# Where VectorE's small work stands: block table one unit tile later, first batch's routing and halving behind a product

## The chip, the cores and the metric

The kernel runs on one core of one Trainium2 chip. The metric is the device time of one execution in microseconds; the median of several runs counts. Matrix products run on TensorE, elementwise work and reductions on VectorE, activations and many casts on ScalarE, some elementwise work and the indirect transfers on GpSimd, and most transfers are issued by SyncE (SP).

## The reference, cut to what matters

The input x has 4 batches of 512 rows of 512 numbers; a context has 4 batches of 512 rows of 256. Cross attention is added to x, and then a mixture-of-experts layer, both behind a layer norm:

```
x = x + xattn(layernorm(x), ctx)     # softmax((ctx Wq+bq)(ctx Wk+bk)^T), times the normed rows
x = x + ffn(layernorm(x))
# ffn(h): logits = h gate_w^T; top 2 of 8 experts by softmax, weights renormalized
#   routed : sum over the 2 experts of  w * (silu(h Wg) * (h Wu)) Wd      (inner width 352)
#   shared : sigmoid(h sgw) * (silu(h Sg) * (h Su)) Sd                    (inner width 1408)
```

## The kernel before, in words

Numbers are split into a high and a low half of 16 bits, and each product takes three matmuls per chunk (high-high, high-low, low-high), so a product of 128 x 512 over a depth of 512 is 12 matmuls.

Up to about 48 us the attention of batches 0 and 1 is computed. Then `ffn_block(t)` runs the shared expert for t = 0 to 3, one batch each, in 11 unit tiles j of 128 columns. For each tile TensorE does the gate product (gate(j)), the up product (up(j)) and, for the tile two before, the down product (down(j-2)). ScalarE applies the SiLU to the gate; VectorE multiplies it with the up product (`product(j)`, L1313); ScalarE casts the high half (L869) and VectorE subtracts for the low half (`low_part`, L1318). TensorE's up(j+1) waits for product(j), since both use one bank. Behind the four blocks come 39 blocks of 128 routed rows each (`expert_product`, `expert_down`), whose rows come back from DRAM sorted by expert; GpSimd adds each block's result to the output by an indirect transfer (L657).

Each engine walks through its own program in order. Everything that isn't the shared expert is hung on points of this walk: the tables `AT_POINT_FIRST` (t = 0), `AT_POINT` (t = 1 and 2) and `AT_POINT_LAST` (t = 3) map (j, "gate" | "up" | "down") to stages, and the same tables are read by every engine, which does its part of the stage there and leaves out stages in which it has no part. On VectorE the order within tile j is: stages of "gate", product(j), stages of "up", low_part(j), stages of "down".

The stages that matter here:

- `logits_before` in block 0: TensorE's 32 small matmuls for the router of batch 0, VectorE's `read_logits` (L1026), ScalarE's exponential, VectorE's `route` (L1036, some twenty small instructions that choose the top two experts and write the weights beside the rows).
- `x_low` in block 0: VectorE scales the last rows of batch 1's attention (L982) and makes four low halves `x_low(1, c)` (L961) from banks of PSUM. TensorE's `turn_attn(1, c)` (L1433, 16 transposes behind up(1)) writes the same banks, each group of four behind its x_low, and VectorE's `attn_low` (L987) reads them.
- `halves_before`: ScalarE's `halve_high(0)` (L752) and VectorE's `halve_low(0)` (L1015) make the two halves of batch 0's normed rows, which GpSimd's `send_rows(0)` scatters to DRAM.
- `assign`: TensorE's small sums of the routing mask and VectorE's row numbers.
- `tables` in block 3: VectorE's three parts (L1120 to L1173) of the table that tells which rows and which expert each of the 39 blocks has. Part 2 releases `table_ready` and `pads_ready`; GpSimd then sends eight pads (L627), and SP loads the first blocks behind those.
- pieces: the routed experts' weights are loaded in 24 pieces through three places of SBUF (a piece's load waits until the piece before in its place has been taken over), cast by ScalarE (`piece_hi`, L845) and subtracted by VectorE (`piece_low`, L1287). `PIECES_AT` sets them beside the tiles, in block 3 two per tile from 4 at (0, "gate") to 15 at (5, "down"), then one per tile. Pieces of one point come behind the stages of that point.

Of the kernel before, what the change touches and what calls it, by code (L numbers as in the profile page):

```python
# [48 lines left out]

AT_POINT_FIRST = {  # L50
    (0, "gate"): [("logits_before", 0)],
    (0, "up"): [("x_low", 0)],
    (0, "down"): [("halves_before", 0)],
    (1, "gate"): [("attn_lows", 0)],
    (1, "up"): [("attn", 0), ("attn", 1), ("attn", 2), ("attn", 3)],
    (1, "down"): [("assign", 0)],
    (2, "gate"): [("mix", 0), ("mix", 1), ("mix", 2), ("mix", 3)],
    (2, "up"): [("stats2", 0)],
    (3, "gate"): [("norm2", 0)],
    (3, "up"): [("halves", 0)],  # L60
    (8, "up"): [("logits", 0)],
# [3 lines left out]

AT_POINT_LAST = {
    (0, "up"): [("assign", 0)],
    (1, "gate"): [("tables", 0)],
    (1, "down"): [("tables", 1)],
    (2, "gate"): [("tables", 2)],  # L70
}


# [22 lines left out]
def at_point(t):  # L96
    return (AT_POINT_FIRST, AT_POINT, AT_POINT, AT_POINT_LAST)[t]
# [6 lines left out]
def build_xattn_moe(nc, x, ctx_in, w_q, b_q, w_k, b_k, gate_w, w_gate, w_up, w_down,  # L104
# [66 lines left out]
    with ExitStack() as stack:  # L171
# [15 lines left out]
        def att_bank(b, stage, i):  # L187

            if stage == "h":
                return bank[(2, 0, 1, 3)[i]]  # L190
            if four_banks(b, stage):
                return bank[b * 4 + (2 if stage == "qk" else 0) + i]
            return bank[1] if stage == "assign" else bank[i % 2]
# [735 lines left out]
        def _(dve):  # L929
            def statistics(which, b):  # L930

                if which == 1:
                    dve.wait_ge(added, RT * b + RT)
                    nc.vector.memset(carrier[:, 1:2], 0.0)
                for i in range(RT):
                    op = nc.vector.bn_stats(stats[:, which, i, :], row_tile(b, i))  # L936
                op.then_inc(stats_done[which], 1)
                variance(which, b)
# [25 lines left out]
            def row_max(b, n):  # L964
                dve.wait_ge(energy_done, RT * b + n + 1)
                nc.vector.tensor_reduce(neg_max[:, n:n + 1], att_bank(b, "energy", n)[:, :], AX.X, ALU.max,
                                        negate=True).then_inc(max_ready, 1)
# [50 lines left out]
            def step(op, b, k):  # L1018

                op.then_inc(r_step, 1)  # L1020
                dve.wait_ge(r_step, ROUTE_STEPS * b + k)

            def over_tile(a):
                return a[:, :].unsqueeze(2).broadcast_to([P, RT, E])

            def read_logits(b):  # L1026
                dve.wait_ge(logits_done, b + 1)
                parts = att_bank(b, "logits", 0)[:, 0:RT * 3 * NL].rearrange("p (t a e) -> p t e a", t=RT, a=3)
                nc.vector.tensor_reduce(logits[:, :, :], parts, AX.X, ALU.add).then_inc(logits_read, 1)
                dve.wait_ge(logits_read, b + 1)  # L1030
                step(nc.vector.tensor_reduce(top[:, :], logits[:, :, 0:E], AX.X, ALU.max), b, 1)
                nc.vector.tensor_scalar(exp_in[:, :, E], logits[:, :, E], -1.0, None, ALU.mult)
                nc.vector.tensor_tensor(exp_in[:, :, 0:E], logits[:, :, 0:E], over_tile(top),
                                        ALU.subtract).then_inc(exp_in_ready, 1)

            def route(b):  # L1036

                dve.wait_ge(r_exp, b + 1)
                nc.vector.tensor_scalar(gate_den[:, :], exp_out[:, :, E], 1.0, None, ALU.add)
                step(nc.vector.tensor_reduce(soft_sum[:, :], exp_out[:, :, 0:E], AX.X, ALU.add), b, 2)  # L1040
                nc.vector.reciprocal(gate_val[:, b, :], gate_den[:, :])
                step(nc.vector.reciprocal(soft_inv[:, :], soft_sum[:, :]), b, 3)
                step(nc.vector.tensor_tensor(probs[:, :, :], exp_out[:, :, 0:E], over_tile(soft_inv), ALU.mult), b, 4)

                p_other = probs[:, :, :].unsqueeze(2).broadcast_to([P, RT, E, E])
                p_own = probs[:, :, :].unsqueeze(3).broadcast_to([P, RT, E, E])
                nc.vector.tensor_tensor(greater, p_other, p_own, ALU.is_gt)
                step(nc.vector.tensor_tensor(equal, p_other, p_own, ALU.is_equal), b, 5)
                step(nc.vector.tensor_tensor(equal.rearrange("p t e j -> p t (e j)"),
                                             equal.rearrange("p t e j -> p t (e j)"),  # L1050
                                             before[:, :, :].rearrange("p e j -> p (e j)").unsqueeze(1)
                                             .broadcast_to([P, RT, E * E]), ALU.mult), b, 6)
                step(nc.vector.tensor_tensor(greater.rearrange("p t e j -> p (t e j)"),
                                             greater.rearrange("p t e j -> p (t e j)"),
                                             equal.rearrange("p t e j -> p (t e j)"), ALU.add), b, 7)
                step(nc.vector.tensor_reduce(rank[:, :, :], greater, AX.X, ALU.add), b, 8)
                nc.vector.tensor_scalar(mask[:, :, :], rank[:, :, :], TOP_K - 0.5, None,
                                        ALU.is_lt).then_inc(mask_ready, 1)
                step(nc.vector.scalar_tensor_tensor(out=chosen[:, :, :], in0=rank[:, :, :], scalar=TOP_K - 0.5,
                                                    in1=probs[:, :, :], op0=ALU.is_lt, op1=ALU.mult), b, 9)  # L1060
                step(nc.vector.tensor_reduce(top_sum[:, :], chosen[:, :, :], AX.X, ALU.add), b, 10)
                step(nc.vector.reciprocal(top_inv[:, :], top_sum[:, :]), b, 11)
                if b == 0:
                    dve.wait_ge(const_ready, 1)
                nc.vector.tensor_copy(hx[b % 2][:, :, TOKEN:XW],
                                      const_f[:, TOKENS][:, b * RT:(b + 1) * RT].unsqueeze(2)
                                      .broadcast_to([P, RT, XW - TOKEN]))
                step(nc.vector.tensor_tensor(hx[b % 2][:, :, META:META + E], chosen[:, :, :], over_tile(top_inv),
                                             ALU.mult), b, 12)
# [167 lines left out]
            def attention(t, j, point):  # L1237

                b = t + 1
                for stage, i in at_point(t).get((j, point), ()):  # L1240
                    if stage == "stats1":
                        statistics(0, b)
                    elif stage == "norm1":
                        normalize(0, b)
                    elif stage == "energy":
                        row_max(b, i)
                    elif stage == "x_halves":
                        x_row_halve(b)
                    elif stage == "inverse":
                        for n in range(RT):  # L1250
                            inverse_sum(b, n)
                    elif stage == "attn_low":
                        attn_row_low(b, i)
                    elif stage == "attn_lows":
                        for c in range(KC):
                            attn_low(b, c)
                    elif stage == "mix":
                        add_mix(b, i)
                    elif stage == "stats2":
                        statistics(1, b)  # L1260
                    elif stage == "norm2":
                        normalize(1, b)
                    elif stage == "logits":
                        read_logits(b)
                    elif stage == "x_low":
                        scale_attn(b, RT - 1)
                        for c in range(KC):
                            x_low(b, c)
                    elif stage == "logits_before":
                        read_logits(b - 1)  # L1270
                        route(b - 1)
                    elif stage == "halves":
                        halve_low(b)
                    elif stage == "halves_before":
                        halve_low(b - 1)
                    elif stage == "assign":
                        assign(b - 1)
                    elif stage == "tables":
                        tables(i)
                    elif stage == "route":  # L1280
                        route(b)
# [453 lines left out]
```

## Time and profile before

| | |
|---|---|
| time before, median of 3 runs | 689.49 us (689.24 to 690.12) |
| the profiled execution | 687.42 us |
| its span, first to last instruction | 685.7 us |
| mean granted TensorE clock | 0.987 of 2.4 GHz |
| VectorE busy | 300.5 us (44%) |
| ScalarE busy | 228.6 us (33%) |
| GpSimd busy | 161.0 us (23%) |

Times of rows are microseconds from the first instruction. TensorE's own rows are of two kinds, PE (matmuls) and PEld (weight loads). A row of a timeline merges like instructions that follow one another: start, length, engine, line, operation, output and inputs, count, and in brackets the idle time before it and what ended it.

### The profile page before, as it was taken

The numbers are of one execution on the slowest core, as the hardware profiler recorded it, in microseconds if no ns is written. First come the engines' busy times: TensorE is split into PE (matmuls) and PEld (weight loads), VectorE is DVE, ScalarE is ACT, GpSimd is POOL, SyncE is SP. The second block draws the span as 40 slices with busy tenths as digits, with TensorE's granted clock in tenths as the row PEclk, the third lists the DMA queues.
The fourth block names the chain that finished last, engine by engine and source line by source line (L and its number), as shares of the span: only waits on it lengthen the run. The fifth ranks groups of instructions, "written<-read, shape, count | busy, mean of one in ns | idle before, by whom it ended". The sixth has DMA issues, their size and how long they took to land.

```text
span 685.7 us, 10319 instructions
## 1 busy us (share of the span) xinstructions
PE 652.5 (95%) x3426; PEld 332.2 (48%) x3426; DVE 300.5 (44%) x703; ACT 228.6 (33%) x341; POOL 161.0 (23%) x134
## 2 busy tenths in 40 slices
PE   8889999999999999999999799999999999999990
PEld 5544444444444444444444344455555555555550
DVE  3899554525524445523559763452222222222220
ACT  3445053313710223620345353332223222223220
POOL 2560280005000004000435700013222222222221
PEclk9999999999999999999999999999999999999995
DMA  9531097222420314430367987348888888888852
GB/s 279 182 92 47 12 307 224 85 93 110 101 39 0 63 32 156 96 60 0 61 210 264 282 276 169 105 117 128 131 128 132 134 129 135 135 126 139 122 72 31
DMA packets 146899, 85.77 MB, mean 125 GB/s; under 512 B 109721, under 2 KB 131481, under 8 KB 146850
## 3 DMA queue, kind: packets, MB, share of 16 engines
q1 hardware_dynamic: 134722, 56.25, 36.0%
q0 software_dynamic: 10544, 27.30, 17.9%
q10 hardware_dynamic: 1584, 1.57, 0.7%
q8 instruction: 31, 0.51, 0.3%
q14 instruction: 18, 0.15, 0.1%
HBM read 32.76 MB, written 27.29 MB: 88 GB/s over the span
## 4 chain that ended last, share of the span: by engine, by line
PE 70%; issue 10%; DMA 7%; DVE 7%; SPq 1%; POOLq 1%; ACT 1%; POOL 1%; ACTq 0%
PE bank L1593 30%; PE bank L1608 16%; PE bank L1641 9%; PE bank L1668 6%; PE bank L1450 5%; DMA out<-staging,token_blk 4%; DMA hidden<-hT 2%; PE bank L1407 2%; DMA arena<-x 1%; PE bank L1416 1%; POOLq L652 1%; DVE arena L955 1%; DVE stats L936 1%; DVE arena L1287 1%; POOL out L657 1%
## 5 line engine op out<-in xcount | busy, mean ns | idle before, releaser
L1593 PE MATMUL bank<-hT,arena 128*128 128x512 f16 x1056 | 238.0, 379 | 5.7 <-DVE prod L1313 4.8
L1593 PEld LDWEIGHTS bank<-hT,arena 128*128 128x128 bf16 x1056 | 102.5, 98 | 132.0 <-DVE prod L1313 6.2
L1641 PE MATMUL bank<-arena,hx_odd 128*128 x936 | 146.0, 313 | 0.0
L1608 PE MATMUL bank<-arena,hidden 128*128 128x512 bf16 x528 | 120.3, 379 | 0.0
L1641 PEld LDWEIGHTS bank<-arena,hx_odd 128*128 128x128 f16 x936 | 91.1, 98 | 53.8 <-issue 0.9
L657 POOL DMA_INDIRECT out<-staging,token_blk x39 | 60.8, 1558 | 165.1 <-ACT staging L913 139.0
L1350 DVE TENSOR_TENSOR prod<-silu_sb,bank 128x352 f32<-128x352 f32 x39 | 20.3, 521 | 150.7 <-PE bank L1641 150.7
L1668 PE MATMUL bank<-arena,hidden 128*128 (+1 forms) x351 | 82.3, 379 | 4.1 <-DMA hidden<-hT 2.5
L1608 PEld LDWEIGHTS bank<-arena,hidden 128*128 128x128 bf16 x528 | 51.3, 98 | 63.0 <-issue 2.3
L875 ACT ACTIVATE silu_sb<-bank 128x512 f32<-128x512 f32 x44 | 26.2, 596 | 112.1 <-PE bank L1593 112.0
L1313 DVE TENSOR_TENSOR prod<-silu_sb,bank 128x512 f32<-128x512 f32 x44 | 30.1, 684 | 75.4 <-PE bank L1593 71.3
L869 ACT CAST hidden<-prod 128x512 bf16<-128x512 f32 x44 | 27.0, 618 | 88.9 <-DVE prod L1313 88.9
L1668 PEld LDWEIGHTS bank<-arena,hidden 128*128 128x128 bf16 (+1 forms) x351 | 34.2, 98 | 41.8 <-issue 7.2
L913 ACT ACTIVATE staging<-bank,w_blk 128x512 f32<-128x512 f32 x39 | 26.8, 687 | 64.6 <-PE bank L1668 64.6
L1318 DVE TENSOR_TENSOR hidden<-prod,hidden 128x512 bf16<-128x512 f32 x44 | 35.0, 799 | 28.7 <-ACT hidden L869 28.5
L609 POOL TENSOR_TENSOR rstd<-var_eps,minus_half 128x4 f32<-128x4 f32 x8 | 9.7, 1207 | 155.7 <-DVE var_eps L949 155.5
L1450 PE MATMUL bank<-arena 128*128 128x512 f16 x192 | 43.1, 379 | 0.0
L901 ACT CAST hT<-prod 128x352 bf16<-128x352 f32 x38 | 18.4, 484 | 63.5 <-DVE prod L1350 63.5
L1287 DVE TENSOR_TENSOR arena<-staging,arena 128x1408 bf16<-128x1408 f32 (+1 forms) x14 | 23.5, 1680 | 15.5 <-ACT arena L845 15.3
L1450 PEld LDWEIGHTS bank<-arena 128*128 128x128 f16 x192 | 18.8, 98 | 23.0 <-issue 0.6
L845 ACT CAST arena<-staging 128x1408 bf16<-128x1408 f32 (+1 forms) x18 | 25.0, 1396 | 9.8 <-DMA staging<-L_ffn_w_gate 7.1
L892 ACT ACTIVATE silu_sb<-bank 128x352 f32<-128x352 f32 x39 | 18.1, 463 | 28.9 <-PE bank L1641 28.9
(190 smaller groups left out, 506.3 us busy)
## 6 DMA issues: line engine op xcount, KB each, us to landing
staging<-L_ffn_w_gate SPq DMA_DIRECT2D x6, 704.0 KB, 4.9
staging<-L_ffn_w_up SPq DMA_DIRECT2D x6, 704.0 KB, 5.9
arena<-x SPq DMA_DIRECT2D x3, 1024.0 KB, 7.4
out<-arena POOLq DMA_DIRECT2D x3, 1024.0 KB, 4.8
staging<-L_ffn_w_down SPq DMA_DIRECT2D x6, 512.0 KB, 3.8
staging<-L_ffn_sw_gate SPq DMA_DIRECT2D x11, 256.0 KB, 3.3
staging<-L_ffn_sw_up SPq DMA_DIRECT2D x11, 256.0 KB, 3.9
staging<-L_ffn_sw_down SPq DMA_DIRECT2D x11, 256.0 KB, 4.5
```

The costliest lines, as they stand in the source:

```text
L657: nc.gpsimd.indirect_dma_start(out=out[:, :], out_offset=bass.IndirectOffsetOnAxis(ap=token_blk[:, k:k + 1], axis=0), in_=yblk[:, k % 2, : ...
L869: nc.scalar.copy(hidden[:, j % 3, HI, :], prod[:, j % 2, :]).then_inc(hid_hi, 1)
L875: nc.scalar.activation(silu_sb[:, :], gate_ps[:, :], ACT.Silu).then_inc(silu_ready, 1)
L913: nc.scalar.activation(yblk[:, k % 2, :], bank[4 + k % 2][:, :], ACT.Copy, scale=w_blk[:, k:k + 1]).then_inc(y_ready, 1)
L1287: nc.vector.tensor_tensor(arena[:, at + gap:at + gap + n], piece_space[piece_slot(q)][:, 0:n], arena[:, at:at + n], ALU.subtract).then_inc ...
L1313: nc.vector.tensor_tensor(prod[:, j % 2, :], silu_sb[:, :], up_ps[:, :], ALU.mult).then_inc(prod_ready, 1)
L1318: nc.vector.tensor_tensor(hidden[:, j % 3, LO, :], prod[:, j % 2, :], hidden[:, j % 3, HI, :], ALU.subtract).then_inc(hid_lo, 1)
L1450: op = nc.tensor.matmul(att_bank(b, "mix", i)[:, :], place(b).xnT[:, xp, c, i * P:(i + 1) * P], place(b).attnT[:, ap, c, :], start=(c == 0 ...
L1593: op = nc.tensor.matmul(ps[:, :], weights[:, j, wp, kind, c * P:(c + 1) * P], hT[:, t % 2, hp, c, :], start=(c == 0 and s == 0), stop=(c = ...
L1608: op = nc.tensor.matmul(out_ps[i][:, :], hidden[:, j % 3, hp, i * P:(i + 1) * P], weights[:, j, wp, DOWN, :], start=(j == 0 and s == 0), s ...
L1641: op = nc.tensor.matmul(ps[:, 0:I], xT[:, k % X_SLOTS, xp * KC + c, :], arena[:, bass.ds(at + (part_at(0, part) + wp * low_gap(part) + c * ...
L1668: op = nc.tensor.matmul(ps[:, :], hidT[0:n, k % 3, hp, c * P:(c + 1) * P], arena[0:n, bass.ds(at + (DOWN_AT + wp * DN + c * H), H)], start ...
```

## The change

The first batch's `route` becomes a stage of its own, `route_before`, and moves from in front of product(0) to behind it, ahead of `x_low`. The halving of batch 0's rows moves from the end of tile 0 to the end of tile 2, for ScalarE and VectorE both. In the last block the three parts of the table move: part 0 from (1, "gate") to (1, "down"), part 1 from (1, "down") to (2, "down"), part 2 from (2, "gate") to (3, "down"). No instruction is added or left out.

```diff
 AT_POINT_FIRST = {
     (0, "gate"): [("logits_before", 0)],
-    (0, "up"): [("x_low", 0)],
-    (0, "down"): [("halves_before", 0)],
+    (0, "up"): [("route_before", 0), ("x_low", 0)],
     (1, "gate"): [("attn_lows", 0)],
...
     (2, "up"): [("stats2", 0)],
+    (2, "down"): [("halves_before", 0)],
     (3, "gate"): [("norm2", 0)],
...
 AT_POINT_LAST = {
     (0, "up"): [("assign", 0)],
-    (1, "gate"): [("tables", 0)],
-    (1, "down"): [("tables", 1)],
-    (2, "gate"): [("tables", 2)],
+    (1, "down"): [("tables", 0)],
+    (2, "down"): [("tables", 1)],
+    (3, "down"): [("tables", 2)],
 }
...
                     elif stage == "logits_before":
                         read_logits(b - 1)
+                    elif stage == "route_before":
                         route(b - 1)
```

## Rows read from the trace of the kernel before

**Rows 1.** The page's first part: busy us, share of the span, instructions.
```profile
PE 652.5 (95%) x3426; PEld 332.2 (48%) x3426; DVE 300.5 (44%) x703; ACT 228.6 (33%) x341; POOL 161.0 (23%) x134
```

**Rows 2.** TensorE's waits: who waited for whom, total us, times, longest.
```profile
PE bank L1593 <- DVE prod L1313: 4.8, 3, 3.5
```

**Rows 3.** Timeline of GpSimd in the expert blocks.
```profile
461.69 1.61 POOL L657 DMA_INDIRECT out<-staging,token_blk  x1 [11.78 <-ACT staging L913]
...
674.17 1.56 POOL L657 DMA_INDIRECT out<-staging,token_blk  x1 [4.06 <-DMA out<-staging,token_blk]
```

**Rows 4.** Timeline of TensorE at the start of block 3.
```profile
363.42 7.93 PE L1593 MATMUL bank<-hT,arena 128*128 128x512 f16 x36
371.64 2.77 PE L1593 MATMUL bank<-hT,arena 128*128 128x512 f16 x12 [0.29 <-DVE prod L1313]
...
383.08 2.77 PE L1593 MATMUL bank<-hT,arena 128*128 128x512 f16 x12 [3.49 <-DVE prod L1313]
...
388.27 5.34 PE L1593 MATMUL bank<-hT,arena 128*128 128x512 f16 x24
```

**Rows 5.** Timeline of TensorE at the start of block 0.
```profile
51.67 5.34 PE L1593 MATMUL bank<-hT,arena 128*128 128x512 f16 x24
57.98 2.76 PE L1593 MATMUL bank<-hT,arena 128*128 128x512 f16 x12 [0.98 <-DVE prod L1313]
60.59 1.91 PE L1433 MATMUL bank<-ident,hx_odd 128*128 128x128 f32 x16
...
62.53 2.75 PE L1593 MATMUL bank<-hT,arena 128*128 128x512 f16 x12
...
80.66 5.34 PE L1593 MATMUL bank<-hT,arena 128*128 128x512 f16 x24
```

**Rows 6.** Timeline of VectorE at the start of block 0.
```profile
53.23 0.17 DVE L1039 TENSOR_SCALAR gate_den<-exp_out 128x4 f32<-128x4 f32 x1 [0.49 <-ACT exp_out L756]
...
57.24 0.69 DVE L1313 TENSOR_TENSOR prod<-silu_sb,bank 128x512 f32<-128x512 f32 x1
...
58.62 2.47 DVE L961 TENSOR_TENSOR arena<-bank,arena 128x512 f16<-128x512 f32 x4
61.02 2.28 DVE L1015 TENSOR_TENSOR arena<-arena 128x2048 f16<-128x2048 f32 x1
...
86.37 0.68 DVE L1313 TENSOR_TENSOR prod<-silu_sb,bank 128x512 f32<-128x512 f32 x1
...
90.62 1.75 DVE L1293 TENSOR_TENSOR arena<-staging,arena 128x1536 bf16<-128x1536 f32 x1
```

**Rows 7.** Timeline of VectorE at the start of block 3.
```profile
367.65 0.16 DVE L1120 TENSOR_TENSOR count<-next_row,const_f 128x8 f32<-128x8 f32 x1
...
369.36 1.62 DVE L1287 TENSOR_TENSOR arena<-hT,arena 128x1408 bf16<-128x1408 f32 x1
...
372.87 0.48 DVE L1135 TENSOR_TENSOR ctx_sb<-const_f,blk_from 128x312 f32<-128x312 f32 x1
...
376.97 1.62 DVE L1287 TENSOR_TENSOR arena<-staging,arena 128x1408 bf16<-128x1408 f32 x1
378.51 0.47 DVE L1150 TENSOR_REDUCE blk_row<-ctx_sb 128x39 f32<-128x312 f32 x1
...
382.34 0.68 DVE L1313 TENSOR_TENSOR prod<-silu_sb,bank 128x512 f32<-128x512 f32 x1
383.70 0.69 DVE L1318 TENSOR_TENSOR hidden<-prod,hidden 128x512 bf16<-128x512 f32 x1 [0.68 <-ACT hidden L869]
```

**Rows 8.** Timeline of ScalarE, the copy of piece 6.
```profile
366.69 1.36 ACT L845 CAST arena<-hT 128x1408 bf16<-128x1408 f32 x1
```

**Rows 9.** Timeline of GpSimd: the first of eight pads.
```profile
381.17 2.08 POOL L627 DMA_INDIRECT xs_dram<-pad_row,pad_idx  x1 [1.75 <-DVE pad_idx L1173]
```

**Rows 10.** DMA issues at 382.45 and 388.37: KB, us from issue to landing.
```profile
staging<-L_ffn_w_up SPq DMA_DIRECT2D x1, 704.0 KB, 5.1
...
staging<-L_ffn_w_up SPq DMA_DIRECT2D x1, 704.0 KB, 10.0
```

## The prediction, made before the kernel was changed

> **What bounds the kernel now.** I read the page's first part, then TensorE's waits, then the chain of waits, then the timelines of the two stretches that the diff touches. TensorE is busy for 652.5 of 685.7 us [rows 1], so a microsecond is won only where TensorE stands still. Its waits name where: its products (L1593) waited three times for VectorE's SiLU product (L1313), 4.8 us in all, 3.5 at the longest [rows 2]. Nothing else that the diff touches makes TensorE wait. Late in the span the chain of waits runs through GpSimd's 39 indirect adds, 5.59 us apart in the mean, from 461.69 to 674.17, the last of which waits for the one before to land [rows 3]. That chain starts from the first expert block, so it is carried forward or back with TensorE and keeps what is won ahead of it.
>
> TensorE issues 12 matmuls in 2.59 us: from 383.08 to 388.27 lie two products, 5.19 [rows 4]. A stall below is a product's start less the place where that rhythm puts it; it is a little more than the idle time printed, since the end of a matmul that is printed lies behind its issue. j is the unit tile of the shared expert, t the block (batch).
>
> **Part 1, the first batch's routing behind the product (t=0).** Before: two products from 51.67 end their issue at 56.85; up(1) starts at 57.98 [rows 5]. The stall is 1.13 us. VectorE shows the cause: route(0) runs from 53.23 to 57.24, 4.01 us, and product(0), on which up(1) waits, follows it [rows 6]. After: product(0) is free to run when up(0) is done, 51.67 + 2.59 and 0.2 to its result, 54.46. It ends at 55.14, and up(1) starts at 56.85. That takes the 1.13 away.
>
> What is late next: route(0) now starts at 55.06 (0.60 from a product to the next instruction), ends at 59.07, and the rest of this point is behind it. The scaling of the last attention row takes 0.78 (57.24 to 58.62 less the product's 0.60), so the four x_low subtractions start at 59.85, 1.23 later than at 58.62 before; each takes 0.60 (58.62 to 61.02 for four), so they end at 60.5, 61.1, 61.7 and 62.3 [rows 6]. TensorE's next work behind up(1) is turn_attn(1), 16 transposes, and its group c waits for x_low(c), since it writes the bank that x_low(c) reads. Before, up(1) gave way at 60.59 and the groups ran unhindered, with the small routing sums behind them, to gate(2) at 62.53: 1.94 us, of which I give 0.2 to the sums and 0.44 to each group [rows 5]. After, up(1) gives way at 59.44, TensorE waits until 60.56 for the first group, the last starts at 62.37, and 0.64 later, at 63.0, gate(2) follows. So the stall is not removed but moved by one product, and made larger: part 1 costs 0.47 us. Bounds: -1.13 (if the transposes were not held) and +1.0 (if each of the four waits cost 0.13 more). I take +0.47, since both lengths are from rows. Behind gate(2) nothing waits: attn_low no longer has halve_low's 2.2 us (from 61.02) in front of it, so it ends nearly 1 us earlier than before, and TensorE has the mix, 48 matmuls, before up(2).
>
> **Part 2, the halving (t=0, from j=0 to j=2).** It takes ScalarE's copy and VectorE's 2.2 us to the place between low_part(2) and the normalization. Product(3) started at 86.37 before [rows 6]; with the 0.47 and 2.28 us more (61.02, its row) it ends at 89.8 at the latest. TensorE needs it at up(4), four products from 80.66, 91.02, plus 0.47: 91.5 [rows 5]. It is hidden by 1.7 us. Behind it on ScalarE are halve_high(1) and the conversions of tiles 5 and 6, on SP the loads of tiles 7 and 8 and the transposes of batch 1; all come at most 2.75 later. The nearest user is gate(5), six products from 80.66, at 96.7 with the 0.47: it needs tile 5, whose subtraction ended at 92.37 (90.62 and 1.75) [rows 6] and now ends by 95.1. GpSimd's sends of batch 0's rows wait for this halving as well; the first to need them sent is ScalarE in the next block. Cost 0, at most 0.5 should a margin be smaller than I put it; a gain is excluded, as nothing waited for the halving at its old place but attn_low, counted above.
>
> **Part 3, the tables (t=3, each part one tile later).** Before: gate(1), up(1) and gate(2) run from 363.42, so up(2) could start at 371.19 and starts at 371.64: 0.45. Three products on, up(3) could start at 379.41 and starts at 383.08: 3.67 [rows 4]. Together 4.12. VectorE is the cause: between product(1) and product(2) stand both tables(1), 372.87 to 376.97, 4.10 us, and tables(2) with a piece, 378.51 to 382.34 [rows 7]. A piece takes 1.54 (376.97 to 378.51), so tables(2) is 2.29; tables(0) is 1.71 (367.65 to 369.36).
>
> After, VectorE's order, on the clock of before, with 1.36 from a product's start to the start of its low part (382.34 to 383.70) and 0.69 for that [rows 7]:
> piece 6 no longer has tables(0) in front but waits for ScalarE's copy, over at 368.05 [rows 8], so 368.08; product(1) 369.62, done at 370.3, and up(2) at 371.19 no longer waits. Low part done 371.7, tables(0) 373.4, pieces 7 and 8 376.5, product(2) done 377.1. Up(3) at 378.96 does not wait (margin 1.8). Low part 378.5, tables(1) 382.6, pieces 9 and 10 385.7, product(3) done 386.4. Up(4), before at 390.86 and now at 386.74, has a margin of 0.3. Low part 387.7, tables(2) 390.0, pieces 11 and 12 393.1, product(4) done 393.8; up(5) at 394.51, margin 0.7. So all of the 4.12 is won, and the tables lie beside TensorE's work at one part per tile. If the first margin fails by as much as a tables step (0.5), 0.2 is lost; lower bound of the gain from this alone is 3.4.
>
> The tables feed more. table_ready comes at about 389; its first user, ScalarE's copy of piece 12, waits until then at least for that piece's load, issued when piece 9 is done at 384.2. The eight pad sends follow the last of it: first at 381.17 [rows 9], then at about 390.3, 9.1 later. SP waits for them before the first blocks of tokens, which TensorE needs only behind block 3, and the loads of pieces 19 to 23 are queued behind those. At 2.08 us each [rows 9] the sends are out by 407 at the latest; piece 19 is used behind gate(9), which by the rhythm (three products a tile) ends near 426. Hidden. But the pads now run beside other loads. A load of a piece took 5.1 us when issued just after the pads started, and 10.0 in their midst and behind another load [rows 10]. The piece that comes just after their new start is 14: issued when piece 11 is done, 391.6, with 5.1 it lands at 396.7, its copy (1.36) and subtraction end at 399.6, product(5) at 400.3, and up(6) is at 402.28. Margin 2.0. With 10.0 product(5) ends at 405.2: 3.0 lost.
>
> The Trainium skill, "DMA: Bandwidth & Descriptors", section "Issuing engines are not separate DMA queues", says that transfers of SP and GpSimd run on the same 16 engines and interleave. The 10.0 beside 5.1 us agrees; by that rule alone, with no part of a load spared, the sum would be that of rival 1.
>
> **Sum.** -4.12 + 0.47 + 0 = -3.65 us. The profiled execution took 687.42, with 685.7 from first to last instruction; it lies 2.07 under the median of the runs, 689.49, and the stalls are part of the program's order, so I take the same difference off the median: 685.8.
>
> **Rivals.**
> 1. The pads take back most of it: piece 14 (or 16) lands as late as the slowest of before, 10.0 us, and up(6) waits 3.0: -0.65, 688.8; at 8.0 us 1.0 is lost, 686.8. For it: that slow load; against it: that one stood right behind another load, and piece 14 is the first of its pair.
> 2. The front is neutral or better: TensorE finds the transposes ready, so 1.13 is won: -5.25, 684.2. Against it are the lengths of route and x_low [rows 6]; it needs route(0) 1 us shorter or more.
> 3. Slower: the same wait at up(6), decided by the landing of piece 14. At 10.7 us after its issue up(6) starts at 405.9, and what is left of the 4.12 is the 0.47 that part 1 costs; each microsecond more is one lost. At 12.5 us it is +1.8, 691.3. No load shown took so long.
> 4. The change does not do what it says: the margin of 0.3 at up(4) is gone because ScalarE's copies of pieces 9 or 10 are late by 2 us; the stall goes from up(3) to up(4), and 1.7 of the 4.12 is lost: -1.95, 687.5. Against it: in the new order their loads are issued earlier than before.
>
> **Chances.** Forecast (685.0 to 686.9) 0.60; rival 1 in full 0.10; rival 2 0.10; rival 3 0.05; rival 4 0.15. The range from 684.6 to 688.2 leaves out rivals 3 and the full 1, and half of 2. What a measurement of this kernel can tell from no change is about 0.2%, 1.38 us. Faster by more than that (below 688.1): forecast, rivals 2 and 4, 0.85. Within it: rival 1 in full, 0.10. Slower: rival 3, 0.05.
>
> **What would show it.** Right: TensorE's wait for the product at up(2) and up(3) of the last block is gone; up(1) of the first block starts 5.2 us after up(0); a new wait of about 1.1 us and three short ones stand in front of the 16 transposes, put down to x_low (L961) or the scaled row (L982); gate(2) is half a microsecond later; the pads start 9 us later. Wrong: a wait for L1313 in front of up(4), up(5) or up(6) of the last block, with ScalarE in front of it waiting for a load; or the transposes running without a wait. The forecast is wrong as a whole if what is won ahead of the expert blocks isn't found at their end.

## The result, and the profile after

| timing | changed kernel, median us | before, median us | ratio | 95% interval |
|---|---|---|---|---|
| first | 683.55 (7 runs) | 689.38 (7) | 0.9922 | 0.9902 to 0.9942 |
| second (`after_again`) | 683.19 (6) | 689.00 (17) | 0.9920 | 0.9898 to 0.9941 |
| third (`after_third`) | 682.74 (6) | 688.26 (17) | 0.9907 | 0.9890 to 0.9924 |

Faster by 5.4, 5.5 and 6.4 us by the ratios. The forecast was 685.8, 3.65 us faster, with a range from 684.6 to 688.2: the right side, too small, and the time is 1.05 us under the range. The profiled execution after took 683.55 us with a span of 681.8; against the profile of before that is 3.87 less, close to the forecast. So the question is why the runs gained more than the two profiles that were compared.

TensorE's waits after (who waited for whom, total us, times, longest), which answer to [rows 2]:

```profile
PE bank L1434 <- DVE arena L961: 1.1, 1, 1.1
PE bank L1408 <- ACT arena L711: 0.8, 1, 0.8
PE bank L1594 <- DVE prod L1314: 0.5, 1, 0.5
```

The three waits for VectorE's product, 4.8 us, are down to one of 0.5, and a wait for x_low (L961) is new. (Line numbers behind the edit are one higher.)

**Part 1.** TensorE's timeline after, at the start of block 0, answers to [rows 5]:

```profile
48.56 2.75 PE L1594 MATMUL bank<-hT,arena 128*128 128x512 f16 x12
51.15 0.95 PE L1471 MATMUL bank<-gw,hT 128*128 128x27 bf16 x32
51.95 7.93 PE L1594 MATMUL bank<-hT,arena 128*128 128x512 f16 x36
60.97 2.36 PE L1434 MATMUL bank<-ident,hx_odd 128*128 128x128 f32 x16 [1.09 <-DVE arena L961]
...
63.37 2.75 PE L1594 MATMUL bank<-hT,arena 128*128 128x512 f16 x12
```

up(0), gate(1) and up(1) now run as one row of 36 matmuls. Then TensorE stands 1.09 us before the transposes, which take 2.36 in place of 1.91, as groups behind the first wait for their x_low too. From gate(0) to gate(2) it is 14.81 us, against 14.26 before (62.53 less the start of gate(0) at 48.27). VectorE's timeline after, for [rows 6], has the reason:

```profile
54.74 0.69 DVE L1314 TENSOR_TENSOR prod<-silu_sb,bank 128x512 f32<-128x512 f32 x1 [1.71 <-PE bank L1594]
55.34 0.16 DVE L1039 TENSOR_SCALAR gate_den<-exp_out 128x4 f32<-128x4 f32 x1
...
60.13 2.48 DVE L961 TENSOR_TENSOR arena<-bank,arena 128x512 f16<-128x512 f32 x4
62.53 2.47 DVE L987 TENSOR_TENSOR arena<-bank,arena 128x512 f16<-128x512 f32 x4
```

The product waits for TensorE, as it should; the routing behind it runs from 55.34 to 59.35, and x_low comes at 60.13.

**Part 3.** TensorE's timeline after, at the start of block 3, for [rows 4]:

```profile
364.25 10.52 PE L1594 MATMUL bank<-hT,arena 128*128 128x512 f16 x48
374.60 2.75 PE L1609 MATMUL bank<-arena,hidden 128*128 128x512 bf16 x12
377.19 5.34 PE L1594 MATMUL bank<-hT,arena 128*128 128x512 f16 x24
382.37 2.75 PE L1609 MATMUL bank<-arena,hidden 128*128 128x512 bf16 x12
384.96 2.75 PE L1594 MATMUL bank<-hT,arena 128*128 128x512 f16 x12
388.23 2.77 PE L1594 MATMUL bank<-hT,arena 128*128 128x512 f16 x12 [0.51 <-DVE prod L1314]
```

The stalls at up(2) and up(3) are gone. One is left at up(4): 384.96 and 2.59 give 387.55, and it starts 0.68 later. Its cause is in ScalarE's and VectorE's rows of this execution (ScalarE first):

```profile
375.41 1.36 ACT L845 CAST arena<-staging 128x1408 bf16<-128x1408 f32 x1 [1.85 <-DMA staging<-L_ffn_w_gate]
...
398.35 1.37 ACT L845 CAST arena<-staging 128x1408 bf16<-128x1408 f32 x1 [0.42 <-DMA staging<-L_ffn_w_gate]
```

```profile
376.80 1.62 DVE L1288 TENSOR_TENSOR arena<-staging,arena 128x1408 bf16<-128x1408 f32 x1 [1.04 <-ACT arena L845]
378.35 0.68 DVE L1314 TENSOR_TENSOR prod<-silu_sb,bank 128x512 f32<-128x512 f32 x1
...
387.50 0.68 DVE L1314 TENSOR_TENSOR prod<-silu_sb,bank 128x512 f32<-128x512 f32 x1
```

The load of piece 8, issued at 368.76, took 6.6 us in this execution, 5.5 in that of before; VectorE stood 1.04 us for it, more than the margin of 0.3 at up(4), and product(3) was late by about the rest. The prediction's walk through VectorE's order gave piece 8 no wait for its load. In the second and third profile of the changed kernel that load took 5.5 and 4.9 us, and up(4) doesn't wait. The second ScalarE row is piece 14, on which rivals 1 and 3 hung: its load landed 4.9 us after its issue at 393.41, beside the pads, whose first send is here:

```profile
392.13 2.08 POOL L627 DMA_INDIRECT xs_dram<-pad_row,pad_idx  x1 [10.11 <-DVE pad_idx L1173]
```

### The profile page after: what moved, and what is told of

The parts are those of the page before. It is cut to its first block, busy times and chain, and to the rows that moved or that the text cites. A ratio compares the mean times of both kernels' runs of the same rounds, so it can differ in the third digit from the quotient of the medians.

```text
span 681.8 us, 10320 instructions
## 1 busy us (share of the span) xinstructions
PE 653.4 (96%) x3426; PEld 333.1 (49%) x3426; DVE 301.3 (44%) x703; ACT 229.1 (34%) x341; POOL 163.6 (24%) x134
## 4 chain that ended last, share of the span: by engine, by line
PE 75%; DVE 8%; DMA 8%; SPq 2%; issue 2%; ACT 1%; POOL 1%; POOLq 0%; ACTq 0%
PE bank L1594 27%; PE bank L1642 16%; PE bank L1609 14%; PE bank L1669 9%; PE bank L1451 5%; DMA hidden<-hT 3%; DMA out<-staging,token_blk 2%; DMA staging<-L_ffn_w_gate 2%; PE bank L1408 1%; SPq L531 1%; DMA arena<-x 1%; PE bank L1417 1%; POOL arena L641 1%; DVE arena L1288 1%; DVE stats L936 1%
```

## The experiments

In all tables and sums below "block 3" is the time from the start of gate(1) of block 3 to the start of the first expert product (L1641), both from TensorE's timeline; "block 0" is the time from gate(0) to gate(2).

**The parts alone, and the kernel before again.** Four kernels on one chip; before: 688.02 us (23 runs).

`tables_only`, only the third part of the diff:

```diff
-    (1, "gate"): [("tables", 0)],
-    (1, "down"): [("tables", 1)],
-    (2, "gate"): [("tables", 2)],
+    (1, "down"): [("tables", 0)],
+    (2, "down"): [("tables", 1)],
+    (3, "down"): [("tables", 2)],
```

> The kernel before with the table's three parts moved alone. Theory A (the prediction's sum holds, and the missing 2 us are a stall that most executions of the kernel before have and the profiled one had not): the time falls by more than part 3's 4.12, by 5.5 to 6.5 against the median of before, because the stall at up(3) of block 3 is larger in most executions than in the one read, and the move takes it away whatever its size. Theory B (the missing 2 us come from the first block, where the move of the routing wins in most executions): it falls by 3.4 to 4.1, no more. Theory C (spread of the runs): by 3.4 to 4.1, and the changed kernel's own gain comes out near 3.6 when taken again. Profile by all: wait for L1313 at up(3) gone, at most 0.7 us left at up(4).

Measured: 683.10 us, ratio 0.9932 (0.9912 to 0.9951): 4.7 us faster, between A's numbers and those of B and C, with an interval (3.4 to 6.1) wide enough for all. Block 3 took 80.29 us, block 0 14.27.

`front_only`, the changed kernel with `AT_POINT_LAST` as before:

> The kernel with the routing behind the product and the halving at j=2, the table where it was. Theory A and C: +0.5 us against before (wait of about 1 us in front of the transposes in place of 1 us in front of up(1), gate(2) half a microsecond later), the 4 us stall of block 3 still there. Theory B: 1 to 2 us faster than before. If the halving at j=2 costs anything, a wait shows at up(4) or gate(5) of block 0.

Measured: 689.40 us, ratio 1.0016 (0.9996 to 1.0035): 1.1 us slower by the ratio, 0.3 faster to 2.4 slower by the interval. Block 0 took 14.80 us. Theory B is out: the front doesn't win. Block 3 took 85.05 us: the gap before up(3) is there, and behind it the product at a granted clock of 1.00 (the column before the last two of the second row), and up(5) stalls 0.61.

```profile
382.92 2.76 PE L1594 MATMUL bank<-hT,arena 128*128 128x512 f16 x12 [3.50 <-DVE prod L1314]
```

```profile
382.92:385.52 2.60, 2.60 (x13) 1.19 (x14) 1.40 (x2) 2.60 (x4) 1.99 (x3) 1.00 0.87 194
```

`xlow_first`, the changed kernel with one list turned round:

```diff
-    (0, "up"): [("route_before", 0), ("x_low", 0)],
+    (0, "up"): [("x_low", 0), ("route_before", 0)],
```

> The changed kernel with x_low ahead of the routing at the same point. If the 0.5 us of part 1 is the four transposes waiting for x_low behind the routing, the wait of 1.1 us in front of them is gone, gate(2) of block 0 starts about 1.5 us earlier after gate(0) than in the changed kernel, and the time falls by 1.5 against it (about 682.0). The routing sums then wait for the mask instead, at most 0.3 us. If something else holds the transposes, nothing changes.

Measured: 682.15 us, ratio 0.9919 (0.9901 to 0.9936). Block 0 took 13.43 us, 1.38 less than in the changed kernel. The timeline of TensorE in the second profile of it (`xlow_again`, below):

```profile
47.44 2.75 PE L1594 MATMUL bank<-hT,arena 128*128 128x512 f16 x12
...
50.83 7.93 PE L1594 MATMUL bank<-hT,arena 128*128 128x512 f16 x36
58.60 1.91 PE L1434 MATMUL bank<-ident,hx_odd 128*128 128x128 f32 x16
60.68 0.18 PE L1498 MATMUL bank<-mask,earlier 128*128 128x32 bf16 x1 [0.17 <-DVE mask L1057]
...
60.88 2.75 PE L1594 MATMUL bank<-hT,arena 128*128 128x512 f16 x12
```

The transposes follow up(1) at once and take 1.91 again; the routing sums wait 0.17 for the mask. So the wait that replaced the one removed came from the order of x_low and the routing.

`before_again`, no edit:

> The kernel before, unchanged, for a second profile of it and the size of the noise. Ratio 1.000. Theory A: this profile, if its time is near the median of 689.4, shows stalls at up(2) and up(3) of block 3 of 5 to 6 us together in place of 4.12. Theories B and C: they are 4.1 again, and the difference to 687.4 lies elsewhere (the loads at the start, the chain of adds at the end).

Measured: 688.80 us, ratio 0.9999 (0.9982 to 1.0015); the profiled execution took 688.99. Its block 3 took 85.92 us, against 84.42 in the profile that the prediction was read from. But its idle times are the same, so A's reason is wrong and its size right. TensorE's timeline:

```profile
373.10 2.76 PE L1593 MATMUL bank<-hT,arena 128*128 128x512 f16 x12 [0.30 <-DVE prod L1313]
...
384.55 4.25 PE L1593 MATMUL bank<-hT,arena 128*128 128x512 f16 x12 [3.50 <-DVE prod L1313]
388.64 2.75 PE L1608 MATMUL bank<-arena,hidden 128*128 128x512 bf16 x12
```

The gap is 3.50 us as in [rows 4]; the twelve matmuls behind it took 4.25 in place of 2.77. The stretches around it, of the profile of before first and then of this one (stretch, its length, busy time of each engine, granted clock, DMA share, GB/s):

```profile
379.42:383.08 3.66, 0.17 (x2) 0.01 (x1) 3.40 (x12) 0.03 (x1) 1.91 (x2) 1.00 0.87 236
383.08:385.68 2.60, 2.60 (x13) 1.19 (x13) 1.40 (x2) 2.60 (x4) 1.99 (x3) 1.00 0.83 181
```

```profile
380.88:384.55 3.67, 0.17 (x2) 0.01 (x1) 3.40 (x12) 0.03 (x1) 1.92 (x2) 0.95 0.83 229
384.55:388.64 4.09, 4.09 (x13) 1.57 (x14) 2.77 (x3) 3.60 (x4) 3.17 (x4) 0.63 0.92 258
```

In the first the granted clock stays at 1.00. In the second it falls: 0.95 over the gap and 0.63 over up(3), a mixture of the two levels, 1.2 and 2.4 GHz. The share of the DMA engines rose as well, from 0.83 to 0.92, but the clock accounts for the whole length: 4.09 us times 0.63 is 2.58, against 2.60 times 1.00, and in all the slow products below the same sum gives 2.5 to 2.6. Theory D is read from this: the gap costs its length, and in some executions the clock behind it.

**The gap longer and shorter.** Before: 689.00 us (17 runs), on one chip with `after_again` and `before_third`.

`gap_long`, the kernel before with

```diff
+                    for n in range(3):
+                        nc.vector.tensor_reduce(delay[:, n:n + 1], row_tile(3, n), AX.X, ALU.max)
                     nc.vector.tensor_tensor(begun, block_no(), over_blocks(blk_from[:, :]), ALU.is_ge)
```

> The kernel before with three more reductions of VectorE (1.8 us, results unused) in front of product(2) of block 3, so that TensorE's gap before up(3) grows from 3.5 to about 5.3 us of idle time. Theory D (in the second profile of before the granted clock fell after the 3.5 us gap and up(3) took 4.25 in place of 2.77 us; the gap is where the clock just falls or just doesn't): now the granted clock falls in every execution, up(3) takes 4 us or more, and the time is 1.8 plus up to 1.5 us above a before whose clock held: about 2.5 us above the median of before. Rival E (the slow up(3) of that profile was an accident of that execution): +1.8 us, up(3) 2.77 us, granted clock 1.00.

Measured: 690.68 us, ratio 1.0021 (1.0007 to 1.0034), 0.5 to 2.3 us slower: E's 1.8 lies within, D's 2.5 just outside. The profile speaks for D. Timeline and stretches (line numbers three higher):

```profile
385.70 5.04 PE L1596 MATMUL bank<-hT,arena 128*128 128x512 f16 x12 [5.31 <-DVE prod L1316]
390.58 2.75 PE L1611 MATMUL bank<-arena,hidden 128*128 128x512 bf16 x12
```

```profile
380.22:385.70 5.48, 0.17 (x2) 0.01 (x1) 5.18 (x16) 0.03 (x1) 1.90 (x1) 0.80 0.50 155
385.70:390.58 4.88, 4.88 (x13) 1.70 (x14) 3.56 (x3) 3.61 (x4) 3.66 (x5) 0.52 0.83 253
```

The clock fell within the gap and stayed at its lower level (0.52) through nearly all of up(3).

`gap_short`, the kernel before with part 2 of the table at tile 3 alone:

```diff
-    (2, "gate"): [("tables", 2)],
+    (3, "down"): [("tables", 2)],
```

> The kernel before with part 2 of the table alone moved to tile 3: product(2) comes 2.29 us earlier and the gap before up(3) shrinks to about 1.2 us of idle time. Theory D: the granted clock stays at 1.00 in up(3), and the gain against the median of before is 2.29 plus the mean cost of the clock, 2.8 to 3.5 us. Rival E: 2.3 us.

Measured: 684.43 us, ratio 0.9936 (0.9920 to 0.9951), 4.4 us faster (3.4 to 5.5). E's 2.3 lies outside the interval, and of D's 2.8 to 3.5 only the upper end within. Timeline and stretch of up(3):

```profile
381.18 2.76 PE L1593 MATMUL bank<-hT,arena 128*128 128x512 f16 x12 [1.20 <-DVE prod L1313]
```

```profile
381.18:383.78 2.60, 2.60 (x12) 1.19 (x13) 1.40 (x2) 2.36 (x3) 0.00 (x0) 1.00 0.91 344
```

Block 3 took 82.13 us, 1.84 over the 80.29 of a block without stalls; 4.12 less 2.29, the length of part 2, is 1.83. More was won than the part's length.

Both times come out lower than D's numbers, and both are taken against the same 17 runs of before. Against each other they leave those out: the medians of `gap_long` and `gap_short` are 6.25 us apart, and block 3 is 6.39 longer in the profile of the first (88.52 and 82.13). By E it would be the idle time alone, 1.8 and 2.29, 4.1 us; even the fastest run of the one and the slowest of the other are 4.19 apart (689.43 and 685.24). E is out.

`before_third` and `before_fourth`, two more profiles of the kernel before:

> The kernel before, a third profile. Theory D: the idle time before up(3) of block 3 is 3.5 us again, and up(3) takes either 2.77 us at a granted clock of 1.00 or about 4.2 us at less; nothing between the start of block 3 and the expert blocks differs otherwise by more than 0.7 us. Rival E: 2.77 us.

> The kernel before, a fourth profile. Idle time before up(3) of block 3 3.5 us; up(3) takes 2.77 us at a granted clock of 1.00, or 4.2 to 4.5 us below it.

Measured: 688.82 and 689.49 us. Block 3 took 86.11 and 86.10. The gap is 3.50 us in both; up(3), from the one and then the other:

```profile
383.77 4.45 PE L1593 MATMUL bank<-hT,arena 128*128 128x512 f16 x12 [3.50 <-DVE prod L1313]
```

```profile
383.64 4.24 PE L1593 MATMUL bank<-hT,arena 128*128 128x512 f16 x12 [3.50 <-DVE prod L1313]
```

Every timed run lists its mean granted clock, so the runs without a profile can be asked too. It is 0.983 to 0.986 in the ten runs of `gap_long`, 0.988 to 0.992 in the five of `gap_short` and in the 19 of the changed kernel, and 0.983 to 0.992 in 69 runs of the kernel before: 48 of these have 0.987 or less and take 689.07 us in the mean, 21 have 0.988 or more and take 687.33. So the kernel before is spread over both kinds. A single run can't be sorted by this number: the execution that the prediction was read from has 0.987, and `before_third`, whose clock fell, 0.988.

**The halving alone, and the turned order again.** Before: 688.26 us (17 runs), on one chip with `before_fourth`.

`halves_only`, the kernel before with

```diff
-    (0, "down"): [("halves_before", 0)],
...
+    (2, "down"): [("halves_before", 0)],
```

> The kernel before with part 2 alone: batch 0's halving at the end of tile 2 in place of tile 0, the routing and the table where they were. By the prediction 0: gate(0) to gate(2) of block 0 14.27 us as before, no wait at up(4) or gate(5), ratio 1.000 within 0.2%. Rival: a margin was smaller than put, and a wait of up to 0.5 us shows there.

Measured: 688.00 us, ratio 0.9994 (0.9980 to 1.0008). Block 0 took 14.36 us, 0.1 more than before; the wait for product(0) has it (1.08 in place of 0.98), which comes ahead of both places of the halving. No wait shows at up(4) or gate(5), and from gate(2) of block 0 to gate(1) of block 3 it is 300.88 us, as in the kernel before. The halving is hidden in the profile; the time leaves room for 0.6 us. Its block 3, 87.09 us, has the same 3.5 us gap with the lower clock at its plainest, in the gap, through up(3), and back behind it:

```profile
378.93:382.59 3.66, 0.16 (x2) 0.01 (x1) 3.40 (x12) 0.02 (x1) 1.91 (x2) 0.81 0.81 234
382.59:387.68 5.09, 5.09 (x12) 1.79 (x13) 3.77 (x3) 3.61 (x4) 3.87 (x5) 0.50 0.92 275
387.68:390.44 2.76, 2.76 (x14) 1.23 (x13) 1.55 (x3) 1.79 (x2) 2.15 (x3) 0.94 0.98 261
```

Granted clock 0.50 is 1.2 GHz; the product took 5.09 us in place of 2.60, 2.5 us for one product.

`xlow_again`, `after_third` and, above, `after_again`:

> The changed kernel with x_low ahead of the routing, again, now beside the changed kernel itself on one chip. By the profiles it should be 1.37 us faster than that (13.44 against 14.81 from gate(0) to gate(2)); rival: the runs' spread hides it or the time is given back later, and the two ratios are the same within 0.1%.

> The changed kernel, third timing and profile. Ratio 0.992 as in the two before. Block 3 from gate(1) to up(10): 69.9 us, or up to 0.7 more where piece 8's load is late; granted clock 1.00 there.

> The changed kernel, unchanged, timed again with more runs of before. If the first measurement was a chance draw, the ratio comes out near 0.9945 (3.65 us); if part 3 is worth more than the 4.12 us of the one profile read, at or under 0.993 (4.8 us or more). Profile: part 1 costs 0.55 again (gate(0) to gate(2) of block 0 14.8 us against 14.27).

Measured: `xlow_again` 681.83 us, ratio 0.9906 (0.9887 to 0.9924); `after_third` 682.74, 0.9907. Block 0 took 13.44 and 14.81 us, as in the profiles before. The 1.37 us of the profile stand against 0.9 us between the medians and nothing between the ratios, so the time doesn't settle it. The profiles keep it as far as the end of block 3 (80.28 and 80.29 us in both kernels). From the first expert product to the end of the span, though, the two profiles with x_low first take 238.61 and 237.36 us, the three of the changed kernel 236.58 to 236.79: about as much goes again there. `front_only`, with the routing first, takes 239.20, so it may be chance; that is not tested. The ratio of `after_again`, 0.9920 and at most 0.9941, leaves out the 0.9945 of a chance draw, and theory C with it. `after_again` and `after_third` both had a block 3 of 80.29 us, without a stall; in the first of them gate(3) and up(3) run as one row, gate(4) and up(4) as another:

```profile
376.21 5.34 PE L1594 MATMUL bank<-hT,arena 128*128 128x512 f16 x24
...
383.98 5.34 PE L1594 MATMUL bank<-hT,arena 128*128 128x512 f16 x24
```

## Why the prediction was right in kind and too small

The pieces of eleven profiled executions, in us:

| kernel | gap before up(3), idle | up(3) | block 3 | over 80.29 |
|---|---|---|---|---|
| before, the one read | 3.49 | 2.77 | 84.42 | 4.13 |
| before_again | 3.50 | 4.25 | 85.92 | 5.63 |
| before_third | 3.50 | 4.45 | 86.11 | 5.82 |
| before_fourth | 3.50 | 4.24 | 86.10 | 5.81 |
| front_only | 3.50 | 2.76 | 85.05 | 4.76, of it 0.61 at up(5) |
| halves_only | 3.50 | 5.30 | 87.09 | 6.80 |
| gap_short | 1.20 | 2.76 | 82.13 | 1.84 |
| gap_long | 5.31 | 5.04 | 88.52 | 8.23 |
| after | none | 2.75 | 80.97 | 0.68 |
| after_again, after_third | none | 2.75 | 80.29 | 0 |

- Part 1: put at +0.47, measured +0.54 to 0.55 (14.80 and 14.81 against 14.26). The wait moved to the transposes, as the prediction said, and `xlow_first` shows that the order behind the product made it. Rival 2 is out: its 684.2 lies nearest to the time that came, but by chance, as the 1.13 that it hung on was not won.
- Part 2: put at 0; measured 0 within 0.2%, and 0 in the profile behind block 0.
- Part 3: put at -4.12. This is the term that was mis-sized. In the four profiles of before the stalls, with what they do to the product behind them, cost 4.13, 5.63, 5.82 and 5.81, 5.35 in the mean; what is left after is 0.68, 0 and 0, 0.23 in the mean. Part 3 is worth 5.1 us, or 5.8 in the commonest case. The missing 1.0 to 1.7 is TensorE's clock behind the gap, and the one execution that the prediction was read from was the one of four in which it held.
- The sum: the step that failed is "the stalls are part of the program's order, so I take the same difference off the median". The profiled execution lay 2.07 under the median. That was taken for an offset that both kernels have; the larger part of it was this cost, which that execution escaped and the change removes. Against the mean of the other three profiles of before it is 1.68 us shorter: block 3 is 1.62 shorter, gate(0) of block 0 starts 0.90 earlier, and what lies behind block 3 is 0.86 longer. With 5.8 for the commonest case and 0.55 lost in front, 5.25 was to be expected, 684.2 off the 689.49; the three timings give 5.4 (4.0 to 6.8), 5.5 (4.1 to 7.0) and 6.4 (5.2 to 7.6).
- What stays open: the mean of the profiled executions falls by 5.49 (688.68 to 683.19), of which block 3 and block 0 make up 4.57. The remaining 0.9 is in stretches that the change doesn't touch: 0.4 ahead of gate(0), which starts at 47.57 to 49.44 in three profiles of the changed kernel and at 48.27 to 49.73 in four of before, and 0.5 behind block 3, 236.58 to 236.79 and 236.40 to 237.86 us. (So what is won ahead of the expert blocks is found at their end, as the prediction asked.) From gate(2) of block 0 to gate(1) of block 3 it is 300.87 to 300.89 us in all seven. Behind block 3 the length largely goes with TensorE's wait for the transfer hidden<-hT (L1668), 1.2 us in all in the profile with the shortest stretch (`tables_only`, 236.07) and 3.3 in that with the longest (`front_only`, 239.20). With spreads of that size the 0.9 may be chance; it was not tested.
- Rival 4's place was right and its cause not: in one of three profiles up(4) waits 0.68, because piece 8's load, not 9's or 10's, was late. Rivals 1 and 3 didn't come: piece 14's load took 4.9 us beside the pads, near the 5.1 taken as likeliest. The Trainium skill's rule that these transfers share the engines ("DMA: Bandwidth & Descriptors", "Issuing engines are not separate DMA queues") is not contradicted, but it didn't set the time.

The version that turns round x_low and the routing has the lowest medians of those run, 682.15 and 681.83 us, and its block 0 is 0.82 us shorter than that of the kernel before instead of 0.55 longer; by the ratios it isn't told from the changed kernel.

## What to carry to other kernels

The price of a gap on TensorE is its idle time and what the products behind it take: look at the granted clock of the first product after each long gap, in more than one profile, since one execution may show it held. A profiled execution that lies well under the median may have been spared something that costs time in the others; look for it before taking the difference over to the changed kernel. It is no proof: `front_only`'s profile escaped the lower clock and lay at the median of its runs, and `tables_only`'s lay 2.57 us under its median with no such gap in block 3. When small work is moved behind the instruction that waits, look at what else stands behind it at its new place, and put first what the next engine waits for.

## What the runs showed of the hardware

With the same 3.5 us of idle time before up(3), the granted clock held in two profiles (before, front_only) and fell in four (the other three of before, and halves_only). After 1.20 us it held and after 5.31 it fell, in one profile each. The fall came within the gap (0.81 and 0.80 in halves_only and gap_long) or only when the work had begun again: in before_third and before_fourth the gap has 1.00 and up(3) 0.60 and 0.64. The rows of before_third:

```profile
380.10:383.77 3.67, 0.17 (x2) 0.01 (x1) 3.40 (x12) 0.03 (x1) 1.92 (x2) 1.00 0.87 231
383.77:388.05 4.28, 4.28 (x12) 1.62 (x13) 2.96 (x3) 3.60 (x4) 3.37 (x4) 0.60 0.95 262
```

The price in block 3 was 1.5 to 1.7 us in the three profiles of before and 2.7 in halves_only. The Trainium skill, "TensorE: Matmul & The Clock Gate", section "What's actually happening", says that the throttled state is the default and that activity lifts it. The rows agree with the second: 0.50 and 0.52 behind the gap in halves_only and gap_long, then 0.94 and 1.00 over the next product.
